# The two feed-forward phases of a layered kernel rewritten without loops: token shift by scaled copies, mix read from PSUM, x updated in place

## The reference

```
x = x + value_row(layernorm(x))       # one row per sequence, from token 1
x = x + ffn(layernorm(x))
x = x + local_attention(layernorm(x)) # 16 heads, blocks of 128 tokens
x = x + ffn(layernorm(x))             # same weights

def ffn(x):
    x_prev = x shifted by one token (zeros ahead of each sequence)
    xr = mu_r * x + (1 - mu_r) * x_prev
    xk = mu_k * x + (1 - mu_k) * x_prev
    r  = sigmoid(xr @ W_r.T)
    k  = square(relu(xk @ W_k.T))
    return r * (k @ W_v.T)
```

## Time and profile before

| what | value |
| --- | --- |
| median of 3 runs | 1849.65 us (1845.47 to 1850.51) |
| the profiled execution's own time | 1848.39 us |
| its span (first to last instruction) | 1846.6 us, 1.8 us less |
| phase f1 | 0 to about 270 us |
| attention | about 270 to 1606 us |
| phase f2 | about 1606 to 1846.6 us |
| PE busy over the span | 84% |
| DVE, ACT, POOL busy over the span | 83%, 69%, 59% |
| mean granted TensorE clock | 0.947 of full |

### The profile page before, as it was taken

The page is one execution under the profiler, slowest core; times in us unless marked ns, Lnnn a source line. Parts: engine busy times, 40 slices in busy tenths (PEclk is TensorE's granted clock), DMA queues, the critical chain, the costliest instruction groups (busy, mean ns, idle before and its releaser), DMA issues. The chain is left out here.

```text
span 1846.6 us, 46621 instructions
## 1 busy us (share of the span) xinstructions
PE 1542.4 (84%) x16872; PEld 1167.3 (63%) x16872; DVE 1523.8 (83%) x4050; ACT 1282.5 (69%) x2333; POOL 1083.6 (59%) x846
## 2 busy tenths in 40 slices
PE   2788854879899988989999999999989998467887
PEld 1677752556666666766666666666766666366776
DVE  3888753899999989999999999999999998265564
ACT  1656641787877878787787887878778878065554
POOL 3678742565665656665665665666656664145554
PEclk8889977999999999999999999999999999788898
DMA  5122111688998999998998999999999989502211
GB/s 177 50 73 89 65 60 37 134 149 152 179 167 164 163 173 165 172 174 150 184 161 167 176 165 172 169 171 179 164 169 156 182 151 166 123 23 80 81 68 69
DMA packets 738474, 252.51 MB, mean 137 GB/s; under 512 B 703824, under 2 KB 723024, under 8 KB 738256
## 3 DMA queue, kind: packets, MB, share of 16 engines
q1 hardware_dynamic: 736736, 248.46, 69.8%
q10 hardware_dynamic: 1520, 1.18, 0.2%
HBM read 48.25 MB, written 25.17 MB: 40 GB/s over the span
## 5 line engine op out<-in xcount | busy, mean ns | idle before, releaser
L1215 ACT ACTIVATE at_prob<-at_prob,at_top 128x256 f32<-128x256 f32 x1024 | 435.9, 497 | 103.9 <-DVE at_top L1083 98.7
L1083 DVE CUSTOM_DVE_ANT_0 at_prob<-at_s_ps,at_masks,pre_s_scale 128x256 f32<-128x256 f32 x1024 | 428.6, 479 | 15.7 <-PE at_s_ps L1433 1.4
L1339 PE MATMUL at_pr_ps<-at_xt,pre_w_h 128*128 128x512 f16 x1024 | 300.2, 386 | 22.7 <-DMA at_xt<-at_x_halves 20.2
L1094 DVE TENSOR_TENSOR at_halves<-at_prob,at_halves 128x1024 f16<-128x1024 f32 x256 | 313.7, 1241 | 2.4 <-ACT at_halves L1225 2.4
L1027 POOL TENSOR_TENSOR at_c_halves<-at_ctx,at_c_halves 128x1024 f16<-128x1024 f32 x64 | 136.5, 2133 | 283.9 <-DVE at_halves L1094 271.1
L1433 PE MATMUL at_s_ps<-at_kt,at_qt 32*128 32x256 f32 x4096 | 259.4, 389 | 48.1 <-DVE at_top L1083 23.2
L1433 PEld LDWEIGHTS at_s_ps<-at_kt,at_qt 32*128 32x128 f32 x4096 | 208.1, 186 | 109.1 <-issue 106.4
L1225 ACT ACTIVATE at_halves<-at_prob 128x1024 f16<-128x1024 f32 x256 | 269.6, 1053 | 6.1
L1396 PE MATMUL at_c_ps<-at_v_h,at_pt 128*128 128x65 f16 x2048 | 215.0, 195 | 66.3 <-DMA at_pt<-at_halves 38.5
L1396 PEld LDWEIGHTS at_c_ps<-at_v_h,at_pt 128*128 128x128 f16 x2048 | 187.2, 98 | 125.3 <-DMA at_pt<-at_halves 65.2
L996 POOL TENSOR_TENSOR at_kt<-at_k_by 128x512 f32<-128x512 f32 x128 | 163.2, 1275 | 110.4 <-DVE at_halves L1094 110.3
(11 more groups left out here) (132 smaller groups left out, 3324.5 us busy)
## 6 DMA issues: line engine op xcount, KB each, us to landing
f_x_raw<-in_x SPq DMA_DIRECT2D x16, 512.0 KB, 4.2
x_after_ffn<-f_x_new SPq DMA_DIRECT2D x16, 512.0 KB, 3.2
at_x_ln<-x_after_ffn SPq DMA_DIRECT2D x16, 512.0 KB, 5.0
at_x_res<-x_after_ffn SPq DMA_DIRECT2D x64, 128.0 KB, 3.1
x_after_attention<-at_x_res SPq DMA_DIRECT2D x64, 128.0 KB, 2.9
f_x<-x_after_attention SPq DMA_DIRECT2D x16, 512.0 KB, 4.4
out_x<-f_x_new SPq DMA_DIRECT2D x16, 512.0 KB, 3.2
at_tables<-in_cos SPq DMA_DIRECT2D x16, 256.0 KB, 4.1
```

Of the source, the lines that this page charges most:

```text
L1083: last = nc.vector.tensor_tensor_reduce(out=prob[:, n % 2, h, :], in0=s_ps[:, h, n % 2 * 2 * P:(n % 2 + 1) * 2 * P], in1=masks[:, kind, :] ...
L1094: nc.vector.tensor_tensor(halves[:, n % HB, 1, :, :], prob[:, n % 2, :, :], halves[:, n % HB, 0, :, :], ALU.subtract).then_inc(p_low, 1)
L1215: last = nc.scalar.activation(prob[:, n % 2, h, :], prob[:, n % 2, h, :], ACT.Exp, bias=top[:, n % 2, h:h + 1], scale=-1.0)
L1339: last = nc.tensor.matmul(pr_ps[:, half, :].rearrange("p (b t) -> p b t", b=SB), w[wp][:, k, at:at + P], xt[:, r, xp, :, k, :], start=n == ...
```

## The change

`ffn_phase` is written anew. The main points:

- No loops: every engine's part is a list of turns, `for c in RUN`, from 4 turns ahead of chunk 0 to one behind chunk 15. A call for a chunk that isn't real gives nothing.
- Token shift: `xt` and `step` are gone. ACT copies `t_ps` four times per chunk (two matrices m, two halves k), each scaled by 1 - mu and one column to the right, into `behind` (L409). DVE makes mix = t_ps * mu + behind, with `t_ps` read from PSUM (L332). POOL has no part in it.
- x is updated in place: six buffers instead of four and no `x_raw`, `x_new`; DVE adds the value row in f1 (L299), POOL adds the gated product (L257), SP fetches chunk c+4 (L213).
- `xn`, `stats`, `mv`, `rstd`, `shift`, `mix_h`, `mix_l`, `gate` and `gated` have two buffers instead of one.
- PE's turn is: keys of c, transposes of c+1 for k=0, receptance of c, transposes of c+2 for k=1, values of c.
- The side work moves to other turns: reductions on DVE in turns 1 and 2, the scale in turn 5, casts on ACT in turns 6, 8, 10, 12, and their rests on DVE one turn later.

The core of the diff (`real(c)` guards and buffer declarations cut):

```diff
-            for s in range(SLOTS if value is None else 2):
-                fetch(s, s)
...
-                    if value is None and before(b, s) and remain(b, s, 3):
-                        fetch(c + 3, (s + 3) % SLOTS)
+            for c in RUN:
+                store(c - 1)
+                fetch(c + AHEAD)
+                if side is not None:
+                    side.sync(sp, c)
...
+            for c in RUN:
+                std_of(c + 3)
+                add_gated(c, 1)
+                add_gated(c, 0)
...
+                    nc.vector.scalar_tensor_tensor(mix[:, m, k, :], t_ps[:, k, :], mu[:, m, k:k + 1],
+                                                   behind[:, m, k, at:at + N], ALU.mult,
+                                                   ALU.add).then_inc(mix_made, 1)
...
+            for c in RUN:
+                mixed(c + 1, K, 0)
+                mixed(c + 1, R, 0)
+                shift_of(c + 2)
+                take(c + 3)
+                low_of(c + 1, K)
+                low_of(c + 1, R)
+                moments(c + 3)
+                gate_value(c, 1)
+                mixed(c + 2, K, 1)
+                mixed(c + 2, R, 1)
+                gate_value(c, 0)
+                if side is not None:
+                    side.vector(dve, c)
...
-            def transposed(c, s):
...
-                nc.scalar.activation(xt[:, s % 2, :, 1:N + 1], t_ps[:, :, :], ACT.Copy).then_inc(xt_made, 1)
+                    nc.scalar.activation(behind[:, m, k, at:at + N], t_ps[:, k, :], ACT.Copy,
+                                         scale=mu_rest[:, m, k:k + 1]).then_inc(behind_made, 1)
...
+            for c in RUN:
+                relu_of(c, 0)
+                edge(c + 1)
+                behind_of(c + 1, K, 1)
+                behind_of(c + 1, R, 1)
+                relu_of(c, 1)
+                behind_of(c + 1, R, 0)
+                square_of(c, 1)
+                behind_of(c + 1, K, 0)
+                square_of(c, 0)
+                high_of(c + 1, K)
+                high_of(c + 1, R)
+                normalize(c + 2, 1)
+                sigmoid_of(c, 1)
+                normalize(c + 2, 0)
+                sigmoid_of(c, 0)
+                if side is not None:
+                    side.scalar(act_e, c)
...
-            def transposes(c):
-                pe.wait_ge(xn_made, c + 1)
-                need(xt_made, c)
+            def transposes(c, k):
+                if real(c):
+                    pe.wait_ge(xn_made, 2 * (c + 1))
+                    need(mix_made, done(c - 1, MIX_NTH[R, k], 4))
...
+            for c in RUN:
+                keys_of(c, 0)
+                keys_of(c, 1)
+                transposes(c + 1, 0)
+                receptance(c, 1)
+                receptance(c, 0)
+                transposes(c + 2, 1)
+                values(c, 1)
+                values(c, 0)
```

More of the change, by code:

```diff
@@ L126, in ffn_phase @@
         v_ps = bank("v_ps")
[L128 to L131, removed]
+        moved = [sem(f"x{s}_moved") for s in range(SLOTS)]
+        ready = sem("ready")
         wv_in = sem("wv_in")
@@ L235, in _, with fetch @@
-            over_batches(batch)(sp)
-            sp.wait_ge(x_made, CHUNKS)
-            store(CHUNKS - 1, 1)
-            for s in range(2):
-                sp.wait_ge(stored[s], 16 * CHUNKS // 2)
+                sp.dma_start(xn[:, 0, :, :], x_in[1, 0:NBLK:BPB, :].partition_broadcast(P)).then_inc(value_in, 16)
+            def fetch(c):
+                if real(c):
+                    need(moved[c % SLOTS], stores(c - SLOTS))
+                    sp.dma_start(x[:, c % SLOTS, :, :], chunk(x_in, c)).then_inc(moved[c % SLOTS], 16)
@@ L429, in _, with take @@
-            over_batches(batch)(dve)
-            gate_value(CHUNKS - 1)
+            def take(c):
+                if value is not None and real(c):
+                    dve.wait_ge(moved[c % SLOTS], loads(c))
+                    dve.wait_ge(vb_made, c // CPB + 1)
+                    row = vb[:, c // CPB, :].unsqueeze(1).broadcast_to([P, CB, C])
+                    nc.vector.tensor_tensor(x[:, c % SLOTS, :, :], x[:, c % SLOTS, :, :], row,
+                                            ALU.add).then_inc(valued, 1)
@@ new lines, in high_of, with normalize @@
+            def high_of(c, m):
+                if real(c):
+                    act_e.wait_ge(mix_made, done(c, MIX_NTH[m, 0], 4))
+                    need((r_done, k_done)[m], done(c - 2, 1, 2))
+                    nc.scalar.activation(mix_h[:, c % 2, m, :, :], mix[:, m, :, :], ACT.Copy).then_inc(high_made, 1)
+            def normalize(c, part):
+                if real(c):
+                    act_e.wait_ge(shift_made, c + 1)
+                    need(t_done, last_first(c - 2, 0))
+                    if value is not None and c == 0:
+                        act_e.wait_ge(va_t, BATCH)
+                    for j in (2 * part, 2 * part + 1):
+                        last = nc.scalar.activation(xn[:, c % 2, j, :], x[:, c % SLOTS, j, :], ACT.Identity,
+                                                    bias=shift[:, c % 2, j:j + 1], scale=rstd[:, c % 2, j:j + 1])
+                    last.then_inc(xn_made, 1)
@@ L557, in values @@
+            def values(c, h):
+                if real(c):
+                    pe.wait_ge(act_made, last_first(c, 0))
+                    need(gated_made, last_first(c - 1, h))
+                    if weights is not None and c == 0:
+                        pe.wait_ge(wv_in, 16)
                     for j in range(2):
```

546 lines of the change are left out of this document (216 added, 330 removed).

## The result

The changed kernel takes 1960.77 us (median of 4 runs, 1958.37 to 1963.38) against 1849.88 beside it. The ratio is 1.0605 with a 95% interval of 1.0582 to 1.0628: slower by 6%. The forecast was 1923 us with a range to 1950, so the sign and the mechanism held, and the size that I gave was 38 us too small: the measured time lies 11 us beyond the range.

The account below looks back on a forecast made before the run. A loop of engine orders bounds the feed-forward turn: 14.3 us plus 2.0 for the clock, P = 16.3. Span 1465.2 + 28P = 1921.6, plus 1.8 around it: 1923 us, range 1868 to 1950.

Parts of the forecast that it names:

- the sign: Whole kernel: slower than before by more than about 0.3% (5.5 us), chance 0.93.
- the mechanism: Feed-forward phases: values and next keys stand behind PE's transposes of c+2, whose `xn` waits on ACT behind work of c+1.
- The floor of 14.3 us per turn: Feed-forward phases: shortest possible turn at the full clock, although no engine is busy for more than 9.9 us of it.
- steps 1 to 7: Feed-forward turn: PE transposes k=0, ACT copies, DVE mix, ACT high parts, ACT normalizes, PE's 4.1 us wait, PE's products; 14.3 us.
- attention and the start of f2: Attention and the opening of the second feed-forward phase: length unchanged at 1345.1 us.
- the start and the filling: f1's first transposes at about 33.1 us; filling each feed-forward phase, from its first transposes on, 9.1 us.
- The clock's term: PE in each feed-forward turn: products behind the wait run at a lower clock, costing 2.0 us per turn.
- The way back: PE, from transposes k=1 to the next k=0: transposes 0.43, values 3.27, keys 2.89 us at the full clock.
- The side work: DVE in f1: reductions, rests, scale and biases lengthen the loop by 20 us, between 10 and 25.
- my own rival "dearer": Feed-forward phases: DVE or ACT operations cost more than assumed, turn 17.3 to 18.3 us, time 1951 to 1979 us; chance 0.12.
- The fetch of x, POOL and SP cost nothing: Feed-forward phases: DVE's wait for x goes; POOL's adds and SP's stores have a whole turn, cost 0.

## Why the prediction was right, and where it fell short

The mechanism was right; what failed are terms of the sum. The floor of 14.3 us per turn (steps 1 to 7) was in fact 14.8; attention and the start of f2, put at no change, took 9.8 us more; the start and the filling were 8.6 short. The clock's term was near, though not for the reason that I gave.

- **The loop, steps 1 to 7: right.** Its seven steps are seen one behind the other in the rows of PE, ACT and DVE above, and moving the values ahead of the waiting transposes took the whole slowdown and more away.
- **Its length: 0.5 us too short, the largest error, about 16 us over 28 turns.** From the transposes for k=0 to those for k=1 it is 8.1, forecast 7.7, and nearly all of it arises ahead of the high parts: ACT came to the copies at 1.0 instead of 0.85, the last copy, 0.71 long where I took the relu's 0.6, ended at 2.8 instead of 2.5, and the first high part began at 3.6 instead of 3.25. DVE's mix from PSUM is 0.7 us (two in 1.41), not above the 0.75 that I took. From the high parts to the last normalize it is 4.5 us, as forecast. The way back at the full clock is 6.7, forecast 6.6. The full-clock turn is 14.8 (with PE kept busy), not 14.3.
- **The clock: the size was near, the reason was not right.** I took 2.0 us per turn. In f2 the way back was 8.95 us in the mean, a loss of 2.2, so 0.2 more than I took and 3 us over 14 turns; in f1 it was 8.64, a loss of 1.9. Of the 0.75 us by which f2's turn of 17.05 exceeds 16.3, two thirds are the loop and one third the clock. I had chosen 2.0 by the length of the wait, and that doesn't order the losses: in f1 of the changed kernel a wait of 9.35 us lost 1.4 (8.14 - 6.7), one of 4.72 lost 2.5:

```profile
118.79 1.11 PE L493 MATMUL f_t_ps<-ffn_ident,f_xn 128*128 128x128 f32 x4 [9.35 <-ACT f_xn L425]
...
126.93 0.60 PE L493 MATMUL f_t_ps<-ffn_ident,f_xn 128*128 128x128 f32 x4
...
188.29 1.11 PE L493 MATMUL f_t_ps<-ffn_ident,f_xn 128*128 128x128 f32 x4 [4.72 <-ACT f_xn L425]
...
197.50 0.60 PE L493 MATMUL f_t_ps<-ffn_ident,f_xn 128*128 128x128 f32 x4
```

  The kernel before shows it too: after a wait of 1.87 us the values came 5.30 us behind the transposes (1747.91 to 1753.21), as late as after the 4.67 of the earlier trace rows. That the mean came near 2.0 is in part luck. What sets the loss of one turn stays open.
- **The side work: 17.9 us, forecast 20.** So much longer than 14 times 8.13 the ways from k=0 to k=1 were in f1, its first turn's 1.3 us with it. Fourteen turns of f1 took 252.6 us, 4.4 more than forecast: the loop's 8, less 2 of the side work and 1 to 2 of the clock.
- **The start and the filling: 8.6 us short.** f1's first transposes came 4.7 us late. mu landed late, which I hadn't looked at; I had only taken away POOL's add. From the first transposes of each phase to those of chunk 1 for k=0 it was 1.5 us (f1) and 2.4 us (f2) longer than 12.0.
- **"Attention and the start of f2 keep their length": wrong by 9.8 us.** I held code that isn't touched to be time that isn't touched. The tile `mu_rest` stands in the diff, and its effect, once taken away, gave the time back.
- The sum of these by place: 4.7 (start) + 1.5 (filling of f1) + 4.4 (turns of f1) + 9.8 (attention) + 2.4 (filling of f2) + 11.4 (turns of f2), and 0.7 at the two ends, is 34.9, which is the difference of the spans (1956.5 - 1921.6). No single term decides: without the attention's term the time would have been 1951, just outside the range, which I had let end at 1950 though my own rival "dearer" reached 1979.
- **The fetch of x, POOL and SP cost nothing: right.** DVE waits for no fetch in the middle of the phases, and POOL's adds (1.40 us in the mean) lie beside the loop.

## What to carry to other kernels

Where an engine works in order, look at what stands *behind* a waiting instruction: a prefetch for the chunk after next may stand only where nothing that its own producer needs is behind it; here the second buffer of `xn` didn't help. Price a wait of PE with what rows show behind such waits, as a range and not by the wait's length alone. And when a change adds even a 16-byte tile, compare the untouched phases too, and take the shift out before judging the rest.

## What I had not expected of the hardware

- Tiles shifted by 32 or 64 bytes made the attention phase about 9 to 13 us longer, by 128 bytes 18 us shorter (8 under the other code), by 256 or 512 not clearly different. By the ratios the whole kernel before moved by +8 (32 bytes), +12 (64), -16 (128), 0 (256) and +1 us (512).
- The loss of clock isn't a fixed price for a wait, nor one that grows with it: with the same products behind it, 1.0 us lost nothing, 3.0 us lost between 0 and 3.1 us, 4.6 us lost 2.0 to 2.3 in the turns of f2, and 9.35 us lost 1.4 in f1.
- Constants of a few bytes landed 7 us later (21.97 against 15.14) in the kernel that issues more large loads at its start. Holding back the side work's loads gave 2.0 of it back; 3.4 us lie in their later issue on ACT.
